# Cross-attention kernel: first queries and first key columns spread by transfers, keys projected in three works of up to 482 columns

## The reference

```python
Q = jax.nn.relu(queries @ Wq + bq)
K = jax.nn.relu(keys @ Wk + bk)
V = jax.nn.relu(values @ Wv + bv)          # keys = values = ctx_1024
scores = jnp.einsum('hbqd,hbkd->hbqk', Qh, Kh) * scale
scores = jnp.where(key_mask[None, :, None, :] == 0.0, NEG, scores)
attn = jax.nn.softmax(scores, axis=-1)
attn = attn * q_mask[None, :, :, None]
out = jnp.einsum('hbqk,hbkd->hbqd', attn, Vh)
return out.transpose(1, 2, 0, 3).reshape(B, Sq, D) + queries
```

## Time and profile before

| what | value |
|---|---|
| runs | 361.71, 358.92, 361.8 us; median 361.71 |
| the profiled execution | 359.1 us, its span 357.2 us |
| PE busy | 348.3 us, 98% of the span |
| PE weight loads | 243.5 us, 68% |
| ACT busy | 300.5 us, 84% |
| DVE busy | 236.8 us, 66% |
| granted TensorE clock | full in every slice |

### The profile page before, as it was taken

The page is one execution under the profiler, slowest core; times in us unless marked ns, Lnnn a source line. Parts: engine busy times, 40 slices in busy tenths (PEclk is TensorE's granted clock), DMA queues, the critical chain, the costliest instruction groups (busy, mean ns, idle before and its releaser), DMA issues.

```text
span 357.2 us, 16853 instructions
## 1 busy us (share of the span) xinstructions
PE 348.3 (98%) x6706; PEld 243.5 (68%) x6706; DVE 236.8 (66%) x777; ACT 300.5 (84%) x397; POOL 7.3 (2%) x30
## 2 busy tenths in 40 slices
PE   8799999999999999999999999999999999999994
PEld 5557676776767677676767767676776767677662
DVE  7768786684939568493956849395774939579321
ACT  1578698988889898888989888888988888898993
POOL 6010000000000000000000000000000000000000
PEclk9999999999999999999999999999999999999999
DMA  5947749685754737375473737547373844537000
GB/s 161 340 107 261 249 166 354 187 291 141 276 148 167 216 127 252 91 276 148 167 216 127 253 90 279 145 167 225 131 239 90 289 136 172 174 115 232 10 9 7
DMA packets 40398, 64.55 MB, mean 181 GB/s; under 512 B 28084, under 2 KB 29364, under 8 KB 40372
## 3 DMA queue, kind: packets, MB, share of 16 engines
q1 hardware_dynamic: 39442, 63.26, 55.0%
q10 hardware_dynamic: 930, 0.90, 0.7%
HBM read 13.73 MB, written 0.82 MB: 41 GB/s over the span
## 4 chain that ended last, share of the span: by engine, by line
PE 95%; DVE 2%; ACT 1%; issue 1%; ACTq 0%; DVEq 0%
PE psum L634 36%; PE psum L610 29%; PE psum L556 14%; PE psum L547 13%; PE psum L725 1%; DVE k_raw L836 1%; PE psum L708 1%; PE psum L719 1%; PE psum L720 0%; DVE late_low L1083 0%; ACT probs L515 0%; ACT query_bd L500 0%; DVE k_high L855 0%; PE psum L577 0%; DVE v_biased L879 0%
## 5 line engine op out<-in xcount | busy, mean ns | idle before, releaser
L515 ACT ACTIVATE probs<-psum 121x800 f32<-121x800 f32 x384 | 293.3, 841 | 40.9 <-PE psum L610 40.9
L634 PE MATMUL psum<-probs,values 121*32 121x200 f32 x3072 | 153.6, 333 | 0.0
L634 PEld LDWEIGHTS psum<-probs,values 121*32 121x32 f32 x3072 | 96.0, 110 | 42.1 <-issue 18.7
L610 PEld LDWEIGHTS psum<-query_bd,k_parts 64*121 64x121 f32 x1536 | 91.8, 181 | 45.2 <-issue 37.8
L610 PE MATMUL psum<-query_bd,k_parts 64*121 64x200 f32 x1536 | 115.8, 281 | 1.0 <-DVE v_biased L879 0.8
L836 DVE TENSOR_SCALAR_CACHE_REDUCE k_raw<-psum,bk_sb 128x361 f32<-128x361 f32 (+2 forms) x63 | 37.6, 599 | 79.2 <-PE psum L547 79.2
L556 PE MATMUL psum<-wv_sb,keyT 128*32 128x129 f32 (+1 forms) x1536 | 54.9, 277 | 0.0
L547 PE MATMUL psum<-keyT,wk_mixed 128*32 128x361 f32 (+2 forms) x504 | 51.6, 484 | 0.0
L889 DVE TENSOR_SCALAR values<-v_biased,keep 121x128 f32<-121x128 f32 x192 | 43.2, 283 | 6.3
L556 PEld LDWEIGHTS psum<-wv_sb,keyT 128*32 128x32 f32 (+1 forms) x1536 | 38.0, 108 | 7.2 <-issue 0.9
L879 DVE TENSOR_TENSOR v_biased<-psum,bv_sb 121x384 f32<-121x384 f32 x64 | 35.1, 548 | 0.0
(11 more groups left out here) (81 smaller groups left out, 78.6 us busy)
## 6 DMA issues: line engine op xcount, KB each, us to landing
k_parts<-k_high SPq DMA_DIRECT2D x30, 722.0 KB, 4.5
k_parts<-k_low SPq DMA_DIRECT2D x30, 722.0 KB, 5.5
keyT<-in_ctxT SPq DMA_DIRECT2D x15, 722.0 KB, 4.2
query_rep<-late_high SPq DMA_DIRECT2D x2, 600.0 KB, 7.7
query_rep<-late_low SPq DMA_DIRECT2D x2, 600.0 KB, 7.8
residual<-in_x SPq DMA_DIRECT2D x64, 12.5 KB
k_parts<-k_high SPq DMA_DIRECT2D x2, 480.0 KB, 5.0
k_parts<-k_low SPq DMA_DIRECT2D x2, 480.0 KB, 3.9
```

The lines of the kernel that those rows point to most:

```text
L515: nc.scalar.activation(probs[0:KTILE, u % PROB_SLOTS], scores_ps[0:KTILE, u % SCORE_SLOTS, :, 0:QCOLS], ACT.Exp, scale=SCALE).then_inc(pro ...
L610: mm = nc.tensor.matmul(scores_ps[0:KTILE, u % SCORE_SLOTS, j, n * TCOLS:(n + 1) * TCOLS], k_parts[rows, parity, t, kt * KTILE:(kt + 1) * ...
L634: mm = nc.tensor.matmul(spans[c * VCOLS:(c + 1) * VCOLS, half, :, :, 0:SPAN], values[0:KTILE, parity, kt, half * HALF_PAIRS + c, :], probs ...
```

## The change

1. The selectors go: no L1100 and L1107 on DVE, no L719 and L720 on PE, no L506 on ACT. Batch 0's queries and first 484 key columns are replicated by eight transfers, five from SP and three from ACT. DVE makes the first 484 columns of all three forms before the other 960, and `load_keys(1, 1)` stands behind these transfers in SP's queue.
2. All four value works and all query projections stand before the first scores, in banks 6, 7, 4, 5 and 0, 1, 2. The masks of the queries are read before `finish_keep`.
3. `KPARTS` is 3: every later batch's keys are projected as 482, 482 and 480 columns. `SIDE_WORK` has four value works, three key works and an empty cycle. In batch 0 two cycles hold one work less.
4. One of the three pieces of the first keys is loaded from ACT's queue, and `bq` last.

```diff
-    KPARTS = 4
-    KCOLS = SK // KPARTS
+    KPARTS = 3
+    KCOLS = -(-SK // KPARTS)
-    Q_BANKS = (3, 6, 7, 6)
+    Q_BANKS = (3, 0, 1, 2)
-    V_BANKS = (0, 1, 2, 3)
+    V_BANKS = (6, 7, 4, 5)
...
+        def replicate_first_keys(eng, source, slot):
+            eng.dma_start(k_parts[slot:P:SLOTS, 0, :, 0:FIRST_COLS].bitcast(F32),
+                          source[:, 0:FIRST_COLS].bitcast(F32)).then_inc(first_k_replicated, 16)
+        def replicate_first_queries(eng, source, slot):
+            eng.dma_start(query_rep[slot:P:SLOTS, :, 0:SQ].bitcast(F32), source[:, 0:SQ].bitcast(F32)
+                          ).then_inc(first_q_replicated, 16)
...
-            sp.wait_ge(first_keys_loaded[KCHUNKS - 1], 16)
+            sp.wait_ge(first_k_high, 1)
+            replicate_first_keys(sp, k_high, 0)
+            replicate_first_keys(sp, k_high, 2)
+            sp.wait_ge(first_k_low, 1)
+            replicate_first_keys(sp, k_low, 1)
+            sp.wait_ge(q_split, 1)
+            for n in (2, 3):
+                replicate_first_queries(sp, q_low, n)
             load_keys(1, 1)
...
-            act.wait_ge(first_q_selected, 1)
+            act.wait_ge(q_relued, 2)
+            for n in (0, 1):
+                replicate_first_queries(act, q_high, n)
+            act.wait_ge(first_k_low, 1)
+            replicate_first_keys(act, k_low, 3)
+            relu_queries(1)
+            relu_queries(2)
+            act.wait_ge(first_q_replicated, 16 * SLOTS)
...
-                                     psum[:, Q_SPREAD_BANK, 0:QUADS * SQ].rearrange("p (t q) -> p t q", q=SQ),
+                nc.scalar.activation(query_bd[:, 0, :, h * SQ:(h + 1) * SQ], query_rep[:, :, 0:SQ].bitcast(F32),
                                      ACT.Copy, scale=blockmask[:, h:h + 1]).then_inc(first_q_spread, 1)
-            for t in range(QUADS):
-                act.wait_ge(first_k_selected, t + 1)
-                nc.scalar.activation(k_parts[:, 0, t, 0:BY_COPY], psum[:, K_SPREAD_BANKS[t], 0:BY_COPY],
-                                     ACT.Copy).then_inc(first_k_spread, 1)
+            relu_queries(3)
...
-            SIDE_WORK = tuple((step,) for step in VALUES + KEYS)
-            FIRST_SIDE_WORK = (((0, NEXT),), ((1, NEXT), (2, NEXT)), ((3, NEXT), VALUES[0]), VALUES[1:2],
-                               VALUES[2:3], (VALUES[3], KEYS[0]), KEYS[1:3], (KEYS[3], (ROWS, NEXT)))
+            SIDE_WORK = tuple((step,) for step in VALUES + KEYS) + ((),)
+            FIRST_SIDE_WORK = (((0, NEXT),), ((1, NEXT), (2, NEXT)), VALUES[0:1], VALUES[1:2],
+                               VALUES[2:3], (VALUES[3], KEYS[0]), KEYS[1:2], (KEYS[2], (ROWS, NEXT)))
...
             project_queries(1)
-            first_scores(2)
             project_queries(2)
-            pe.wait_ge(q_relued, QGROUPS - 1)
+            sum_queries(0)
             project_queries(3)
-            sum_queries(0)
+            pe.wait_ge(q_relued, QGROUPS)
+            scores(0, 0, 0)
+            pe.wait_ge(q_relued, 1 + QGROUPS)
+            scores(0, 0, 1)
+            pe.wait_ge(first_evacuated, KCHUNKS + VGROUPS)
+            scores(0, 0, 2)
...
-            center_keys(k_high, 0, k_high_ready)
+            center_keys(k_high, 0, first_k_high, first)
+            center_keys(k_cent, 0, first_k_cent, first)
+            dve.wait_ge(first_k_high, 1)
+            dve.wait_ge(first_k_cent, 1)
+            low_keys(first_k_low, first)
             dve.wait_ge(q_relued, 2)
             low_first_queries(slice(0, SQ))
-            center_keys(k_cent, 0, k_cent_ready)
+            center_keys(k_high, 0, k_high_ready, rest)
+            center_keys(k_cent, 0, k_cent_ready, rest)
```

More of the change, by code:

```diff
@@ L355, in _ @@
             sp.dma_start(wk_sb[:], Wk).then_inc(wk_loaded, 16)
[L356 to L359, removed]
+            load_first_keys(sp, 0)
+            load_first_keys(sp, 2)
             sp.dma_start(wv_sb[:, 0:D], Wv).then_inc(wv_loaded, 16)
             sp.dma_start(bv_sb[:], bv.to_broadcast([P, D])).then_inc(wv_loaded, 16)
-            sp.wait_ge(first_keys_loaded[KCHUNKS - 1], 16)
+            sp.wait_ge(first_k_high, 1)
[6 more added lines that the diff above has]
+                replicate_first_queries(sp, q_low, n)
             load_keys(1, 1)
             sp.wait_ge(k_high_ready, 1)
-            replicate(0, k_high, (0, 2), BY_COPY)
+            replicate(0, k_high, (0, 2), FIRST_COLS)
             sp.wait_ge(k_low_ready, 1)
-            replicate(0, k_low, (1, 3), BY_COPY)
+            replicate(0, k_low, (1, 3), FIRST_COLS)
             sp.wait_ge(pads_zeroed, 4)
@@ L517, in batch @@
                                          ACT.Exp, scale=SCALE).then_inc(probs_ready, 1)
-                    if isinstance(b, int) and b == 0 and u in LATE_QUERIES:
-                        for g in LATE_QUERIES[u]:
-                            relu_queries(g)
             batch(0, 0)
@@ L709, in project_queries @@
                                  start=True, stop=True).then_inc(q_projected, 1)
-            def first_scores(u):
-                if u < EARLY_UNITS:
-                    pe.wait_ge(first_evacuated, KCHUNKS + (u + 1) * HALF_QUADS)
-                scores(0, 0, u)
-            def select(bank, t, high, low, high_kind, low_kind):
-                nc.tensor.matmul(bank, selectors[:, t, high_kind], high, start=True, stop=False)
-                return nc.tensor.matmul(bank, selectors[:, t, low_kind], low, start=False, stop=True)
             pe.wait_ge(ones_ready, 1)
-            for _ in range(WARM_UPS):
-                nc.tensor.matmul(psum[:, Q_SPREAD_BANK, 0:P], ones[:], ones[:], start=True, stop=True)
+            for n in range(WARM_UPS):
+                bank, part = divmod(n % (2 * BANK // P), BANK // P)
+                nc.tensor.matmul((o_ps, work_ps)[bank][:, part * P:(part + 1) * P], ones[:], ones[:],
+                                 start=True, stop=True)
             pe.wait_ge(wk_permuted, 1)
@@ L732, in _ @@
             project_queries(0)
-            def first_values(g):
-                if g < KCHUNKS:
-                    pe.wait_ge(first_evacuated, g + 1)
-                else:
-                    pe.wait_ge(q_relued, 2)
+            pe.wait_ge(wv_loaded, 32)
+            pe.wait_ge(pads_zeroed, 2)
+            for g in range(VGROUPS):
                 for n in range(VGROUP):
@@ L851, in max_keys, with center_keys @@
                 dve.wait_ge(k_max_ready, 2 * b + 2)
-            def center_keys(target, b, done):
-                v.tensor_scalar(target[:, 0:SK], k_raw[:, 0:SK], 0.0, of_batch(k_max, b), ALU.max, ALU.subtract
+            def center_keys(target, b, done, at=slice(0, SK)):
+                v.tensor_scalar(target[:, at], k_raw[:, at], 0.0, of_batch(k_max, b), ALU.max, ALU.subtract
                                 ).then_inc(done, 1)
@@ L981, in first_batch @@
             def first_batch():
-                mask_queries(0)
                 used = SUMS
```

107 lines of the change are left out of this document (38 added, 69 removed).

## The result

The changed kernel takes 368.98 us in the median of 4 runs (367.77 to 369.53), the kernel before 360.45 beside it (4 runs, 358.92 to 361.8). The ratio is 1.023, with a 95% interval of 1.017 to 1.029: it is slower, by about 2%. The ratios of this document are worked out from all runs but those over 1.5% above the fastest of their kernel, and so are not quite those of the medians. I had predicted slower as the likeliest outcome, but 364.5 with a range up to 368. Both the size and the range are wrong, and one of the two large terms is too.

A forecast was written before the change was run, and what follows sets the result against it. PE was taken to bound the middle, a chain of small steps the start. 359.1 + 7.1 - 3.0 = 363.2 us, or 365.8 from the kernel's upper level; 364.5 was predicted, between them, range 360 to 368.

The forecast's parts named there:

- the two large terms: Middle batches: 7.1 us lost to waits behind empty cycles; start of the kernel: 3.0 us gained.
- The empty cycle: Batches 1 to 13: third scores behind it wait for ACT's third exponential, 0.55 us a batch, 7.1 in all.
- half a wait: Rival, middle batches: scores or exponentials start earlier, so the loss is 0.27 x 13 = 3.5 us, total 359.6; chance 0.08.
- no wait: Rival, middle batches: ACT's third exponential ends in time, loss 0, the start's gain stands, 356.1 us; chance 0.10.
- The start's 3.0 us: Batch 0: the third cycle begins at 25.2 instead of 28.18, a gain of 3.0 us.
- the landing of the queries: Start: query copies land 2.7 us after the last issue at 12.3, at 15.0; first scores at 16.2.
- the length of the first cycle: Batch 0: first scores at 16.2, second cycle at 22.2 instead of 25.00.
- The upper bound that I gave: Start: if the 240 KB pieces also take 5.0 us, first scores come at 17.0 and 2.2 us are gained.
- The third cycle: Batch 0: begins at 22.2 + 1.97 + 0.81 + 0.3 = 25.2 us, against 28.18 before.
- Late replicas: Rival, start: copies land late, first scores at 18.2, gain only 1.0 us, 365.2 on the profile's level; chance 0.17.
- the 5.0 us of the earlier trace: Start: four transfers of 480 KB took up to 5.0 us each; batch 0's remaining columns were to land in 5.0.
- The prediction's own test: Wrong if a batch stays 20.8 us, exceeds 21.4, or batch 0's third cycle begins after 27.

The follow-up runs named there:

- the fill: Changed kernel with two unused 128x128 matmuls of constants in each empty cycle; 372.19 us, 1.032 of the kernel before.
- the kernel that has the change and no stops: Changed kernel plus nineteen one-column fills on VectorE and twenty-four one-column matmuls on TensorE; 367.25 us, 1.017 of the kernel before.
- four trivial instructions: Changed kernel with nineteen instead of fifteen unused one-column fills on VectorE; 367.77 us (1.019 of the kernel before) against 370.92 (1.030).
- the kernel before with nine fills: Kernel before with nine unused one-column fills added to VectorE at 2.9 us; 364.72 us, 1.009 of the kernel before.
- the last experiment: Changed kernel with four key works, constant matmuls at the start and residual loads issued behind batch 1's key copies; 358.27 us, 0.995 of the kernel before.
- the new start alone: Changed kernel with four key works of 361 columns and the old side-work lists; 364.81 us, 1.010 of the kernel before.

## Why the prediction was wrong

**The empty cycle** was right in place, cause and size. 7.1 us were forecast, 6.9 measured. Key cycles are 2.77 or 2.78 (forecast 2.78), the empty one 1.97, the batch 21.32 (21.3), and the fill showed that it is a wait. The rivals of half a wait and of no wait are out.

**The start's 3.0 us were wrong**; measured are 0.2. The steps that failed are the landing of the queries and the length of the first cycle:
- First scores at 17.52 instead of 16.2. The queries landed at 16.27, not 15.0: SyncE issued two `k_high` copies in 2.10 (forecast 1.30), two queries in 1.6 and ACT its two in 1.8, with ScalarE's queue issuing beside it, and `k_high` was 0.6 late in this execution. The last is chance: with the same start it came at 9.21 and 8.98 in two others, and their first scores still at 17.16 and 17.50. The upper bound that I gave (17.0, gain 2.2) was thus the better forecast.
- The second cycle 7.62 after the first scores, not 6.0. Of this at least 0.58 is the half clock. I had watched engines for the path, and not what TensorE's longer wait for the copies does to its clock. The kernels with constant matmuls still need 6.3 to 7.0 (6.3 and 6.5 with shorter key works), but the matmuls lengthen it too, so what it would be without them stays open.
- The third cycle 2.89 behind, forecast 3.0: right.
- "Late replicas" (gain 1.0) was the rival nearest to the truth: at full clock the gain is 1.0 and 1.4 (batch 1 at 44.81 and 44.42, with four key works). The nearness is in part luck. Its condition, first scores at 18.2, was not met (16.95 to 17.81 in all profiles of the new start), and the rest is lost in the first cycle. I also read the 5.0 us of the earlier trace rows as a most; it is a median, and the 480 KB pieces took 6.3 and 7.1 after the change.

**Three stops of 4.0 us in sum were missing.** The prediction put them at nothing, without a reason. The change shifted the count of instructions, and for VectorE's stop and TensorE's behind the loop the runs show that this decides on their place; in the kernel before the transfer lay in a wait that hid VectorE's. The cause of the stop ahead of the loop (1.2 us) is open. The range had no room for them: only the kernel that has the change and no stops, with 366.9 in its profiled execution, lies within it. With them and the true start the sum is 359.1 + 6.9 - 0.2 + 4.0 = 369.8, measured 369.5. That the direction came out as forecast rests on the empty cycles, the size on stops that I had not seen.

The prediction's own test, wrong "if batch 0's third cycle begins after 27", was met at 28.03.

## What to carry over

When ACT or another engine needs longer for a cycle than the shortest cycle of the bound engine gives it, evenly spread side work is worth more than fewer, larger works: the total was the same here and 0.53 us a batch went into one wait. A step that makes TensorE wait for a transfer can cost slower work after it, here 0.58 us or more. And before a change of a few microseconds is blamed or praised, look for waits with no releaser around loops: four trivial instructions moved this kernel by 0.4% between two profiled executions and by 0.9% between the medians.

## What was not expected of the hardware

- Stops of 0.82 to 2.33 us on TensorE and of 2.60 to 4.54 on VectorE, ahead of a loop or behind it. In all fifteen the engine went on 1.3 to 1.6 us after a packet of an instruction queue had landed. VectorE's cost TensorE's cycles 1.6 to 3.4 us, with the clock's fall behind some of them; where the transfer fell in a wait of 1.93 us it cost nothing.
- Before the last output the clock was at its lower level for 3.41 us at a time, in three profiled executions for 6.83, mostly in the start or behind a stop. The waits of TensorE before it were short: 1.82 us in the start of after, 1.99 behind VectorE's stop in the kernel before with nine fills, and 1.26 in that kernel's start, which the kernel before has as well, without a fall.
- In the kernel before the 23 runs beside the last experiment stand in groups, and the mean granted clock of each run goes with them: 6 at 359.0 to 359.3 us with 0.998 or 0.999, 10 at 360.9 to 361.4 all with 0.994, 5 at 362.0 to 363.5 with 0.992 to 0.997, 2 at 365.1 to 365.6 with 0.988. 3.41 us at half clock lower the mean of 359 us by 0.005 and can cost 1.7 us, so one such stretch more from the first group to the second is likely; when it comes no profile shows. The two kernels with constant matmuls at the start and four key works have no run above 362.2.
- The issue of one 242 KB transfer on SyncE's queue took 0.60 to 1.05 us while ScalarE's issued too, and 2.16 once (the new start alone).
